# DLRM on one core: filling the gram's slots from the PSUM bank of the transposes in place of the features in SBUF

## The chip, the cores and the metric

The kernel runs on 1 core of a Trainium2 chip. The metric is the time of one execution on the device in microseconds. A run with the profiler gives, beside its time, the span of the profiled instructions.

## What is computed

A recommendation model (DLRM) for 2048 samples: 26 rows are looked up in embedding tables for each sample, a small network gives a 27th vector, the products of all pairs of the 27 vectors are taken, and all of it goes through four dense layers.

```python
B, NF, D, V, NDENSE = (2048, 26, 64, 12500, 13)
h = jax.nn.relu(dense @ dw1 + db1)
dense_emb = jax.nn.relu(h @ dw2 + db2)
sparse_emb = emb_tables[f_ids, sparse_idx]
emb = jnp.concatenate([dense_emb[:, None, :], sparse_emb], axis=1)
inter = jnp.einsum('bfd,bgd->bfg', emb, emb)
pairs = inter[:, iu0, iu1]
z = jnp.concatenate([emb.reshape(emb.shape[0], -1), pairs], axis=1)
z = jax.nn.relu(z @ ow1 + ob1)
z = jax.nn.relu(z @ ow2 + ob2)
z = jax.nn.relu(z @ ow3 + ob3)
return z @ ow4 + ob4
```

## The kernel before

The 2048 samples are 16 tiles of 128. All five engines run one program each, written out by hand; semaphores order them, and within an engine the order of the code is the order of the work.

**GpSimd** issues the gathers (line 212): 26 indirect DMAs a tile, one for each table, each bringing 128 rows of 64 floats into `emb`, a ring of four tiles. Two neighbouring tables lie side by side, so a tile is 13 blocks of 128x128. The blocks are in four groups (`GROUPS`: 4, 4, 4 and 1 blocks), each with its semaphore. Before the gathers of tile t GpSimd waits for the transposes of group 0 of tile t-1.

**TensorE** waits for a group's rows, transposes its blocks (line 540) into `tr_ps`, which has two PSUM banks: groups 0 and 2 use bank 0, groups 1 and 3 bank 1. The features, now 128 features x 128 samples a block, are the weights of layer 1 (line 588, `features1`), which accumulates in `l1_ps`. `gram` (line 567) multiplies samples' slots with themselves for the products. `turn_pairs` transposes the picked pairs of the tile before through bank 0 of `tr_ps`, `pairs1` adds them to layer 1, `turn_hidden1` transposes the layer's result. `upper(b, s)` are the steps of layers 2 to 4 for a batch of tiles and use bank 1 of `tr_ps`. The last tile, 15, has its own order (lines 709 to 736) and its own forms: `last_features1` (line 656), `last_gram` (line 635).

**Evacuation.** ScalarE copies groups 0 and 2 out of `tr_ps` into `feat` (`evac_features`, line 375), VectorE groups 1 and 3 (line 247). For the gram the features are needed a second time, in another layout: `slots[h*64 + d, j, c, f]`, where the 128 samples are split in (c, h, j) and the 27 slots f are next to each other, padded to 32. Slots 0 to 12 are the lower halves (features 0 to 63) of the 13 blocks, slots 13 to 25 the upper halves, slot 26 the dense vector. ScalarE fills the first from `feat` (`even_slots`, line 382), VectorE the second (`odd_slots`, line 254), each in two parts of a tile (`SLOT_PARTS`: blocks 0 to 7 and 8 to 12; three parts in the last tile). A part is two copies, one for each h; each reads single floats that are 128 apart in `feat` and writes runs of as many floats as the part has blocks. Line 434 fills the dense slot.

**Around it.** After the gram ScalarE (line 394) and VectorE (line 278) copy it out of PSUM, VectorE transposes it in 32x32 blocks (line 286; the last tile's straight from PSUM, line 298), ScalarE picks the pairs (`pick_pairs`, lines 400 and 406). `hidden1_turn` (line 266) is VectorE's copy of layer 1's turned result. `result(b)` (line 428) is ScalarE's last step of a batch; `hidden2`, `hidden3` are the ones before.

The semaphores `feat_act` and `feat_dve` count the evacuations, `slots_act` and `slots_dve` the slot parts. TensorE waits for `feat_act` or `feat_dve` before it writes a bank of `tr_ps` again (line 531 in `transposes`, and in `turn_pairs` and `upper`), and for the slots before `gram`.

Of the kernel before, what the change touches and what calls it, by code (L numbers as in the profile page):

```python
# [13 lines left out]
P = 128  # L14
# [1 line left out]
GROUPS = [(0, 4), (4, 8), (8, 12), (12, 13)]  # L16
BATCHES = [(0, 4), (4, 8), (8, 12), (12, 14), (14, 15), (15, 16)]
LAST = BATCHES[-1][0]
SLOT_PARTS = [(0, 8), (8, 13)]
LAST_PARTS = [(0, 8), (8, 12), (12, 13)]  # L20


def bass_dlrm_kernel(
# [18 lines left out]
    D = dw1.shape[1]  # L42
# [21 lines left out]
    with ExitStack() as ctx:  # L64
# [153 lines left out]
        def _(dve):  # L218
# [24 lines left out]
            def evac_features(t, n):  # L243
                a, b = GROUPS[n]
                src = tr_ps[:, n % 2, 0:(b - a) * P].rearrange("p (k c) -> p k c", c=P)
                dve.wait_ge(transposed, t * NG + n + 1)
                nc.vector.tensor_copy(feat[t % 2][:, a:b, :], src).then_inc(feat_dve, 1)  # L247

            def odd_slots(t, a, b):
                dve.wait_ge(feat_act, 2 * t + (1 if b <= 8 else 2))  # L250
                dve.wait_ge(feat_dve, 2 * t + (1 if b <= 12 else 2))
                for h in range(2):
                    src = feat[t % 2][D:P, a:b].rearrange("p k (c h j) -> p h j c k", h=2, j=HALF)[:, h]
                    last = nc.vector.tensor_copy(slots[t % 2][h * D:(h + 1) * D, :, :, NP + a:NP + b], src)  # L254
                last.then_inc(slots_dve, 1)

            def pairs_copy(t):
# [60 lines left out]
            for t in range(LAST):  # L318
                if t >= 1:
                    gram_copies(t - 1, 0)  # L320
                    if end_stage(t - 1) and end_stage(t - 1)[1] == 1:
                        hidden2(end_stage(t - 1)[0])
                    gram_copies(t - 1, 1)
                    turn_gram(t - 1)
                    pairs_copy(t - 1)
                evac_features(t, 1)
                if t >= 1:
                    hidden1_turn(t - 1)
                odd_slots(t, *SLOT_PARTS[0])
                if mid_stage(t) and mid_stage(t)[1] == 1:  # L330
                    hidden2(mid_stage(t)[0])
                evac_features(t, 3)
                odd_slots(t, *SLOT_PARTS[1])
            gram_copies(14, 0)
            gram_copies(14, 1)
            turn_gram(14)
            hidden2(3)
            pairs_copy(14)
            evac_features(15, 1)
            hidden1_turn(14)  # L340
            odd_slots(15, *LAST_PARTS[0])
            odd_slots(15, *LAST_PARTS[1])
            evac_features(15, 3)
            odd_slots(15, *LAST_PARTS[2])
            turn_last_gram()
            pick_high_pairs()
            pairs_copy(15)
# [4 lines left out]
        def _(act):  # L352
# [21 lines left out]
                act.wait_ge(transposed, t * NG + n + 1)  # L374
                nc.scalar.copy(feat[t % 2][:, a:b, :], src).then_inc(feat_act, 1)  # L375

            def even_slots(t, a, b):
                act.wait_ge(feat_act, 2 * t + (1 if b <= 8 else 2))
                act.wait_ge(feat_dve, 2 * t + (1 if b <= 12 else 2))
                for h in range(2):  # L380
                    src = feat[t % 2][0:D, a:b].rearrange("p k (c h j) -> p h j c k", h=2, j=HALF)[:, h]
                    last = nc.scalar.copy(slots[t % 2][h * D:(h + 1) * D, :, :, a:b], src)  # L382
                last.then_inc(slots_act, 1)

            def gram_copies(t, half):
# [89 lines left out]
            for t in range(LAST):  # L475
                if t >= 1:
                    gram_copies(t - 1, 0)
                    if end_stage(t - 1):
                        upper_act(*end_stage(t - 1))
                    gram_copies(t - 1, 1)  # L480
                evac_features(t, 0)
                if t >= 1:
                    pick_pairs(t - 1)
                    hidden1(t - 1)
                dense_slots(t)
                even_slots(t, *SLOT_PARTS[0])
                if mid_stage(t):
                    upper_act(*mid_stage(t))
                evac_features(t, 2)
                even_slots(t, *SLOT_PARTS[1])  # L490
            gram_copies(14, 0)
            hidden2(3)
            gram_copies(14, 1)
            evac_features(15, 0)
            pick_pairs(14)
            hidden1(14)
            dense_slots(15)
            even_slots(15, *LAST_PARTS[0])
            hidden3(3)
            evac_features(15, 2)  # L500
            result(3)
            even_slots(15, *LAST_PARTS[1])
            even_slots(15, *LAST_PARTS[2])
            pick_low_pairs()
            hidden2(4)
            last_hidden1(0)
# [8 lines left out]
        def _(pe):  # L515
# [12 lines left out]
            def transposes(t, n):  # L528
                a, b = GROUPS[n]
                if 2 * t + n // 2 > 0:  # L530
                    pe.wait_ge((feat_act, feat_dve)[n % 2], 2 * t + n // 2)
                if n == 1 and t >= 1 and end_stage(t - 1):
                    pe.wait_ge(upper_out, out_count(end_stage(t - 1)))
                if n == 2 and t >= 1:
                    pe.wait_ge(pairs_in, t)
                if n == 3 and mid_stage(t):
                    pe.wait_ge(upper_out, out_count(mid_stage(t)))
                pe.wait_ge(gathered[t % RING][n], (t // RING + 1) * 32 * (b - a))
                for k in range(a, b):
                    last = nc.tensor.transpose(tr_ps[:, n % 2, (k - a) * P:(k - a + 1) * P], emb[:, t % RING, k, :],  # L540
                                               ident_sb[:])
                last.then_inc(transposed, 1)

            def turn_pairs(t, evacuated):
                pe.wait_ge(feat_act, evacuated)
                if t == LAST:
                    pe.wait_ge(last_picked, 2)
                else:
                    pe.wait_ge(pairs_picked, t + 1)
                for c in range(PC):  # L550
                    mm = nc.tensor.transpose(tr_ps[0:PR, 0, c * P:(c + 1) * P],  # L551
                                             pairs_b[t % 2][:, c * PR:(c + 1) * PR], ident_sb[:])
                mm.then_inc(pairs_turned, 1)

            def gram(t, half):
                if half == 0:
                    pe.wait_ge(dense_slot, t + 1)
                    pe.wait_ge(slots_act, len(SLOT_PARTS) * (t + 1))
                    pe.wait_ge(slots_dve, len(SLOT_PARTS) * (t + 1))
                if 2 * t + half > 0:  # L560
                    pe.wait_ge(gram_act, 2 * t + half)
                    pe.wait_ge(gram_dve, 2 * t + half)
                for j in range(half * HALF // 2, (half + 1) * HALF // 2):
                    for h in range(2):
                        x = slots[t % 2][h * D:(h + 1) * D, j]
                        bank, r = 2 * h + j // SETS % 2, j % SETS
                        mm = nc.tensor.matmul(gram_ps[:, bank, r * GCOLS:(r + 1) * GCOLS],  # L567
                                              x.rearrange("p c f -> p (c f)"), x[:, :, 0:SLOTS],
                                              start=True, stop=True)
                mm.then_inc(gram_done, 1)  # L570
# [33 lines left out]

            def upper(b, s, evacuated):
                n = upper_cols(b)
                pe.wait_ge(feat_dve, evacuated)
                if b + s > 0:
                    pe.wait_ge(upper_out, 4 * b + s)
                if s == 0:  # L610
                    pe.wait_ge(h1t_ready, BATCHES[b][1])
                    if b == 0:
                        pe.wait_ge(w234_in, 48)
                if s in (0, 1):
                    for k in range(M1):
                        mm = nc.tensor.matmul(tr_ps[:, 1, 0:n], w2_sb[:, k, s * P:(s + 1) * P], h1t[b % 2][:, k, 0:n],  # L616
                                              start=(k == 0), stop=(k == M1 - 1))
                    mm.then_inc(l2_done, 1)
                elif s == 2:
                    for k in range(M2):  # L620
                        mm = nc.tensor.matmul(tr_ps[:, 1, 0:n], w3_sb[:, k, :], h2[:, k, 0:n],
                                              start=(k == 0), stop=(k == M2 - 1))
                    mm.then_inc(l3_done, 1)
                else:
                    nc.tensor.matmul(tr_ps[0:1, 1, 0:n], w4_sb[:], h3[:, 0:n], start=True, stop=True).then_inc(l4_done, 1)

            def last_gram():
                pe.wait_ge(dense_slot, LAST + 1)
                pe.wait_ge(slots_act, len(SLOT_PARTS) * LAST + len(LAST_PARTS))
                pe.wait_ge(slots_dve, len(SLOT_PARTS) * LAST + len(LAST_PARTS))  # L630
                for j in range(HALF):
                    for c in range(SETS):
                        for h in range(2):
# [169 lines left out]
```

## Time and profile before

| | us |
|---|---|
| median of 3 runs | 552.72 |
| lowest, highest | 552.71, 553.63 |
| the profiled execution | 554.64 |
| its span | 552.7 |
| TensorE busy (matmul) | 444.2 |
| GpSimd busy | 398.2 |
| ScalarE busy | 159.4 |
| VectorE busy | 141.9 |

Busy time is what an engine's instructions cover; the issuing of a gather on GpSimd counts as busy. The granted TensorE clock of the execution was 0.928 of full speed. A row of the timeline starts with its start and its length in us. An engine that waits names in brackets who released it; "issue" means that nothing in the profile held it. An fp32 matmul of the program stands as two in the trace.

### The profile page before, as it was taken

Reading aid. Unit: us, or ns where it says so; the run is one execution under the profiler, and the core shown is the slowest. Engines: PE = TensorE matmul, PEld = TensorE weight load, DVE = VectorE, ACT = ScalarE, POOL = GpSimd, SP = SyncE. Lnnn points to the kernel's source line nnn. Section 1 sums busy time; section 2 is a strip of 40 time slices with the busy share of each in tenths; the row PEclk is TensorE's granted clock in tenths of the full one; section 3 lists DMA queues with packets and bytes.
Section 4 is the critical chain, followed back from the end, with each engine's and each line's share of the span. In section 5 each row is a group of like instructions: output and inputs, shape, how many; then the busy total and the mean of one; then the engine's idle time right before and its main releaser. Section 6 shows DMA issues by size and latency. Waiting matters only on the chain.

```text
span 552.7 us, 5884 instructions
## 1 busy us (share of the span) xinstructions
PE 444.2 (80%) x2326; PEld 236.6 (43%) x2326; DVE 141.9 (26%) x225; ACT 159.4 (29%) x265; POOL 398.2 (72%) x420
## 2 busy tenths in 40 slices
PE   3757989585887979799685988979597899959978
PEld 1124553252534435354342534525253444525767
DVE  1003324031331223214032231413222123311412
ACT  1303334122232232324133232323333223332322
POOL 5777777777777777777777777777777777777720
PEclk9999999798898979979798998979989799997998
DMA  8633323233332323333232332324333232333310
GB/s 274 133 49 25 29 26 25 27 28 26 27 26 26 27 26 28 26 27 26 26 28 26 27 26 28 27 26 27 26 28 26 26 27 26 27 25 27 26 13 1
DMA packets 17166, 19.38 MB, mean 35 GB/s; under 512 B 7359, under 2 KB 8386, under 8 KB 17127
## 3 DMA queue, kind: packets, MB, share of 16 engines
q0 software_dynamic: 13312, 13.66, 30.5%
q1 hardware_dynamic: 3408, 5.02, 2.7%
q10 hardware_dynamic: 420, 0.34, 0.3%
q8 instruction: 18, 0.29, 0.2%
q14 instruction: 8, 0.07, 0.0%
HBM read 18.99 MB, written 0.01 MB: 34 GB/s over the span
## 4 chain that ended last, share of the span: by engine, by line
POOL 57%; issue 19%; PE 15%; DMA 6%; SPq 1%; ACT 1%; DVE 1%; POOLq 0%; DVEq 0%
POOL emb L212 57%; DMA w1p_sb<-ow_pairs_dram 5%; PE l_ps L588 5%; PE gram_ps L567 2%; PE tr_ps L616 2%; PE l_ps L656 1%; DMA emb<-table_dram,rows 1%; PE gram_ps L656 1%; PE tr_ps L540 1%; PE l_ps L594 1%; PE gram_ps L635 0%; SPq L189 0%; PE l_ps L581 0%; PE gram_ps L663 0%; PE l_ps L663 0%
## 5 line engine op out<-in xcount | busy, mean ns | idle before, releaser
L212 POOL DMA_INDIRECT emb<-table_dram,rows x416 | 398.0, 957 | 130.1 <-issue 125.6
L588 PE MATMUL l_ps<-w_sb,feat 128*128 128x512 f32 x390 | 204.3, 674 | 3.7 <-DVE feat L247 1.5
L588 PEld LDWEIGHTS l_ps<-w_sb,feat 128*128 128x128 f32 x390 | 81.8, 220 | 107.6 <-issue 89.8
L540 PE MATMUL tr_ps<-ident_sb,emb 128*128 128x128 f32 x208 | 39.3, 306 | 62.5 <-DMA emb<-table_dram,rows 61.4
L278 DVE COPY gram_c<-gram_ps 32x432 f32<-32x432 f32 x60 | 36.6, 610 | 138.8 <-PE gram_ps L567 138.4
L382 ACT COPY slots<-feat 64x512 f32<-64x512 f32 (+3 forms) x66 | 58.6, 888 | 45.6 <-DVE feat L247 43.6
L567 PEld LDWEIGHTS gram_ps<-slots 64*128 64x128 f32 x960 | 56.1, 188 | 26.8 <-issue 15.5
L567 PE MATMUL gram_ps<-slots 64*128 64x108 f32 x960 | 61.2, 277 | 6.7 <-DVE gram_c L278 6.7
L394 ACT COPY gram_c<-gram_ps 32x432 f32<-32x432 f32 x60 | 30.6, 509 | 122.4 <-PE gram_ps L567 122.0
L247 DVE COPY feat<-tr_ps 128x512 f32<-128x512 f32 (+1 forms) x32 | 15.7, 492 | 191.4 <-PE tr_ps L540 191.4
L540 PEld LDWEIGHTS tr_ps<-ident_sb,emb 128*128 128x128 f32 x208 | 26.1, 152 | 90.2 <-issue 88.7
L594 PE MATMUL l_ps<-w1p_sb,pairs 118*128 118x512 f32 x90 | 42.6, 610 | 9.8 <-DVE pairs L259 9.8
L375 ACT COPY feat<-tr_ps 128x512 f32<-128x512 f32 x32 | 18.8, 586 | 77.9 <-PE tr_ps L540 77.6
L254 DVE COPY slots<-feat 64x512 f32<-64x512 f32 (+3 forms) x66 | 34.6, 524 | 6.8 <-ACT feat L375 4.2
L411 ACT ACTIVATE h<-l_ps 128x512 f32<-128x512 f32 x15 | 9.0, 598 | 74.5 <-PE l_ps L594 74.5
L616 PE MATMUL tr_ps<-h1t,w_sb 128*128 128x512 f32 (+2 forms) x80 | 28.6, 502 | 0.2 <-ACT h L416 0.2
L286 DVE STREAM_TRANSPOSE gram_b<-gram_c 128x864 f32<-128x864 f32 x15 | 28.1, 1872 | 1.4
L594 PEld LDWEIGHTS l_ps<-w1p_sb,pairs 118*128 118x128 f32 x90 | 15.9, 189 | 27.7 <-issue 14.4
L581 PE MATMUL l_ps<-w1d_sb,dense_e 64*128 64x512 f32 x30 | 17.8, 674 | 8.2 <-DMA w1p_sb<-ow_pairs_dram 8.2
L259 DVE COPY pairs<-tr_ps 118x384 f32<-118x384 f32 x16 | 8.9, 558 | 41.3 <-PE tr_ps L551 41.3
L616 PEld LDWEIGHTS tr_ps<-h1t,w_sb 128*128 128x128 f32 x80 | 14.0, 197 | 10.6 <-issue 9.5
L518 PE MATMUL gram_ps<-dense_sb,dw_sb 13*64 13x512 f32 x8 | 7.1, 1063 | 9.0 <-DMA dw_sb<-dw_dram 9.0
(67 smaller groups left out, 174.9 us busy)
## 6 DMA issues: line engine op xcount, KB each, us to landing
emb<-table_dram,rows POOLq DMA_INDIRECT x416, 3.3
w_sb<-ow_dram SPq DMA_DIRECT2D x3, 1024.0 KB, 9.7
w1p_sb<-ow_pairs_dram SPq DMA_DIRECT2D x1, 708.0 KB
w_sb<-ow_dram SPq DMA_DIRECT2D x1, 512.0 KB, 21.8
w_sb<-ow_dram SPq DMA_DIRECT2D x1, 256.0 KB, 13.0
idx_raw<-idx_dram ACTq DMA_DIRECT2D x1, 208.0 KB, 2.6
w1d_sb<-ow_dram SPq DMA_DIRECT2D x1, 128.0 KB
w_sb<-ow_dram SPq DMA_DIRECT2D x1, 128.0 KB, 6.4
```

What stands on the lines that cost most here:

```text
L212: pool.indirect_dma_start(out=emb[:, t % RING, c // 2, c % 2 * D:(c % 2 + 1) * D], out_offset=None, in_=table, in_offset=bass.IndirectOffs ...
L254: last = nc.vector.tensor_copy(slots[t % 2][h * D:(h + 1) * D, :, :, NP + a:NP + b], src)
L278: last = nc.vector.tensor_copy(dst, src)
L286: nc.vector.transpose(gram_b[t % 2][:, 0:SLOTS, :], gram_c[:].rearrange("p i g -> p g i")).then_inc(gram_turned, 1)
L375: nc.scalar.copy(feat[t % 2][:, a:b, :], src).then_inc(feat_act, 1)
L382: last = nc.scalar.copy(slots[t % 2][h * D:(h + 1) * D, :, :, a:b], src)
L394: last = nc.scalar.copy(dst, src)
L540: last = nc.tensor.transpose(tr_ps[:, n % 2, (k - a) * P:(k - a + 1) * P], emb[:, t % RING, k, :], ident_sb[:])
L567: mm = nc.tensor.matmul(gram_ps[:, bank, r * GCOLS:(r + 1) * GCOLS], x.rearrange("p c f -> p (c f)"), x[:, :, 0:SLOTS], start=True, stop=True)
L588: nc.tensor.matmul(l1_ps[t % 2][:], feat[t % 2][:, n - 1, :], w1_sb[:, n - 1, :], start=False, stop=False)
L594: mm = nc.tensor.matmul(l1_ps[t % 2][:], pairs[t % 2][:, c, :], w1p_sb[:, c, :], start=False, stop=c == PC - 1)
L616: mm = nc.tensor.matmul(tr_ps[:, 1, 0:n], w2_sb[:, k, s * P:(s + 1) * P], h1t[b % 2][:, k, 0:n], start=(k == 0), stop=(k == M1 - 1))
```

## The change

`even_slots` and `odd_slots` are gone, and with them their two parts a tile. In their place stands `group_slots(t, n)`, once on ScalarE and once on VectorE, called right behind `evac_features(t, n)` for the same group. It makes four copies out of the bank of `tr_ps` that was just evacuated: for each half of the partitions (even and odd slots) and each h one. So ScalarE fills all slots of groups 0 and 2, VectorE all of groups 1 and 3. What is read lies again 128 floats apart, now in PSUM; what is written are runs of 4 floats (of 1 in group 3).

TensorE therefore waits for `slots_act` and `slots_dve` where it waited for `feat_act` and `feat_dve` before it writes a bank of `tr_ps`. Layer 1 (`features1`, `last_features1`) still waits for `feat_act` and `feat_dve`. The gram waits for two groups of each engine. TensorE's and GpSimd's instructions and their order stay.

```diff
--- before.py
+++ after.py
@@ -16,8 +16,6 @@
 GROUPS = [(0, 4), (4, 8), (8, 12), (12, 13)]
 BATCHES = [(0, 4), (4, 8), (8, 12), (12, 14), (14, 15), (15, 16)]
 LAST = BATCHES[-1][0]
-SLOT_PARTS = [(0, 8), (8, 13)]
-LAST_PARTS = [(0, 8), (8, 12), (12, 13)]
 
 
 def bass_dlrm_kernel(
@@ -246,12 +244,13 @@
                 dve.wait_ge(transposed, t * NG + n + 1)
                 nc.vector.tensor_copy(feat[t % 2][:, a:b, :], src).then_inc(feat_dve, 1)
 
-            def odd_slots(t, a, b):
-                dve.wait_ge(feat_act, 2 * t + (1 if b <= 8 else 2))
-                dve.wait_ge(feat_dve, 2 * t + (1 if b <= 12 else 2))
-                for h in range(2):
-                    src = feat[t % 2][D:P, a:b].rearrange("p k (c h j) -> p h j c k", h=2, j=HALF)[:, h]
-                    last = nc.vector.tensor_copy(slots[t % 2][h * D:(h + 1) * D, :, :, NP + a:NP + b], src)
+            def group_slots(t, n):
+                a, b = GROUPS[n]
+                for half, base in ((0, a), (1, NP + a)):
+                    src = tr_ps[half * D:(half + 1) * D, n % 2, 0:(b - a) * P].rearrange(
+                        "p (k c h j) -> p h j c k", k=b - a, h=2, j=HALF)
+                    for h in range(2):
+                        last = nc.vector.tensor_copy(slots[t % 2][h * D:(h + 1) * D, :, :, base:base + b - a], src[:, h])
                 last.then_inc(slots_dve, 1)
 
             def pairs_copy(t):
@@ -324,24 +323,23 @@
                     turn_gram(t - 1)
                     pairs_copy(t - 1)
                 evac_features(t, 1)
+                group_slots(t, 1)
                 if t >= 1:
                     hidden1_turn(t - 1)
-                odd_slots(t, *SLOT_PARTS[0])
                 if mid_stage(t) and mid_stage(t)[1] == 1:
                     hidden2(mid_stage(t)[0])
                 evac_features(t, 3)
-                odd_slots(t, *SLOT_PARTS[1])
+                group_slots(t, 3)
             gram_copies(14, 0)
             gram_copies(14, 1)
             turn_gram(14)
             hidden2(3)
             pairs_copy(14)
             evac_features(15, 1)
+            group_slots(15, 1)
             hidden1_turn(14)
-            odd_slots(15, *LAST_PARTS[0])
-            odd_slots(15, *LAST_PARTS[1])
             evac_features(15, 3)
-            odd_slots(15, *LAST_PARTS[2])
+            group_slots(15, 3)
             turn_last_gram()
             pick_high_pairs()
             pairs_copy(15)
@@ -374,12 +372,13 @@
                 act.wait_ge(transposed, t * NG + n + 1)
                 nc.scalar.copy(feat[t % 2][:, a:b, :], src).then_inc(feat_act, 1)
 
-            def even_slots(t, a, b):
-                act.wait_ge(feat_act, 2 * t + (1 if b <= 8 else 2))
-                act.wait_ge(feat_dve, 2 * t + (1 if b <= 12 else 2))
-                for h in range(2):
-                    src = feat[t % 2][0:D, a:b].rearrange("p k (c h j) -> p h j c k", h=2, j=HALF)[:, h]
-                    last = nc.scalar.copy(slots[t % 2][h * D:(h + 1) * D, :, :, a:b], src)
+            def group_slots(t, n):
+                a, b = GROUPS[n]
+                for half, base in ((0, a), (1, NP + a)):
+                    src = tr_ps[half * D:(half + 1) * D, n % 2, 0:(b - a) * P].rearrange(
+                        "p (k c h j) -> p h j c k", k=b - a, h=2, j=HALF)
+                    for h in range(2):
+                        last = nc.scalar.copy(slots[t % 2][h * D:(h + 1) * D, :, :, base:base + b - a], src[:, h])
                 last.then_inc(slots_act, 1)
 
             def gram_copies(t, half):
@@ -479,28 +478,27 @@
                         upper_act(*end_stage(t - 1))
                     gram_copies(t - 1, 1)
                 evac_features(t, 0)
+                group_slots(t, 0)
                 if t >= 1:
                     pick_pairs(t - 1)
                     hidden1(t - 1)
                 dense_slots(t)
-                even_slots(t, *SLOT_PARTS[0])
                 if mid_stage(t):
                     upper_act(*mid_stage(t))
                 evac_features(t, 2)
-                even_slots(t, *SLOT_PARTS[1])
+                group_slots(t, 2)
             gram_copies(14, 0)
             hidden2(3)
             gram_copies(14, 1)
             evac_features(15, 0)
+            group_slots(15, 0)
             pick_pairs(14)
             hidden1(14)
             dense_slots(15)
-            even_slots(15, *LAST_PARTS[0])
             hidden3(3)
             evac_features(15, 2)
+            group_slots(15, 2)
             result(3)
-            even_slots(15, *LAST_PARTS[1])
-            even_slots(15, *LAST_PARTS[2])
             pick_low_pairs()
             hidden2(4)
             last_hidden1(0)
@@ -528,7 +526,7 @@
             def transposes(t, n):
                 a, b = GROUPS[n]
                 if 2 * t + n // 2 > 0:
-                    pe.wait_ge((feat_act, feat_dve)[n % 2], 2 * t + n // 2)
+                    pe.wait_ge((slots_act, slots_dve)[n % 2], 2 * t + n // 2)
                 if n == 1 and t >= 1 and end_stage(t - 1):
                     pe.wait_ge(upper_out, out_count(end_stage(t - 1)))
                 if n == 2 and t >= 1:
@@ -542,7 +540,7 @@
                 last.then_inc(transposed, 1)
 
             def turn_pairs(t, evacuated):
-                pe.wait_ge(feat_act, evacuated)
+                pe.wait_ge(slots_act, evacuated)
                 if t == LAST:
                     pe.wait_ge(last_picked, 2)
                 else:
@@ -555,8 +553,8 @@
             def gram(t, half):
                 if half == 0:
                     pe.wait_ge(dense_slot, t + 1)
-                    pe.wait_ge(slots_act, len(SLOT_PARTS) * (t + 1))
-                    pe.wait_ge(slots_dve, len(SLOT_PARTS) * (t + 1))
+                    pe.wait_ge(slots_act, 2 * t + 2)
+                    pe.wait_ge(slots_dve, 2 * t + 2)
                 if 2 * t + half > 0:
                     pe.wait_ge(gram_act, 2 * t + half)
                     pe.wait_ge(gram_dve, 2 * t + half)
@@ -604,7 +602,7 @@
 
             def upper(b, s, evacuated):
                 n = upper_cols(b)
-                pe.wait_ge(feat_dve, evacuated)
+                pe.wait_ge(slots_dve, evacuated)
                 if b + s > 0:
                     pe.wait_ge(upper_out, 4 * b + s)
                 if s == 0:
@@ -626,8 +624,8 @@
 
             def last_gram():
                 pe.wait_ge(dense_slot, LAST + 1)
-                pe.wait_ge(slots_act, len(SLOT_PARTS) * LAST + len(LAST_PARTS))
-                pe.wait_ge(slots_dve, len(SLOT_PARTS) * LAST + len(LAST_PARTS))
+                pe.wait_ge(slots_act, 2 * LAST + 2)
+                pe.wait_ge(slots_dve, 2 * LAST + 2)
                 for j in range(HALF):
                     for c in range(SETS):
                         for h in range(2):
```

On VectorE, in tile 1 of the program, before (`COPY slots<-feat` is `odd_slots`, `h1t` is `hidden1_turn`):

```order
L247 COPY feat<-tr_ps 128x512
L266 COPY h1t<-l_ps 128x4x128
L254 COPY slots<-feat 64x64x8 x2
L247 COPY feat<-tr_ps 128x128
L254 COPY slots<-feat 64x64x5 x2
```

and now:

```order
L245 COPY feat<-tr_ps 128x512
L253 COPY slots<-tr_ps 64x64x4 x4
L265 COPY h1t<-l_ps 128x4x128
L245 COPY feat<-tr_ps 128x128
L253 COPY slots<-tr_ps 64x64 x4
```

The copies read `tr_ps`, there are eight and not four, and `hidden1_turn` stands behind the first four.

On ScalarE, in the last tile, before (`COPY gram_b` and `pairs_b` are `pick_pairs(14)`, `ACTIVATE y` is `result(3)`, the `ACTIVATE h` of 128x256 is `hidden3(3)`):

```order
L375 COPY feat<-tr_ps 128x512
L400 COPY gram_b<-gram_b 128x13x13
L406 COPY pairs_b<-gram_b 128x351
L411 ACTIVATE h_0<-l_ps 128x512
L434 COPY slots<-dense_e 64x64 x2
L382 COPY slots<-feat 64x64x8 x2
L422 ACTIVATE h<-tr_ps,bias_sb 128x256
L375 COPY feat<-tr_ps 128x512
L428 ACTIVATE y<-tr_ps,bias_sb 1x256
L382 COPY slots<-feat 64x64x4 x2
L382 COPY slots<-feat 64x64 x2
```

and now:

```order
L373 COPY feat<-tr_ps 128x512
L381 COPY slots<-tr_ps 64x64x4 x4
L399 COPY gram_b<-gram_b 128x13x13
L405 COPY pairs_b<-gram_b 128x351
L410 ACTIVATE h_0<-l_ps 128x512
L433 COPY slots<-dense_e 64x64 x2
L421 ACTIVATE h<-tr_ps,bias_sb 128x256
L373 COPY feat<-tr_ps 128x512
L381 COPY slots<-tr_ps 64x64x4 x4
L427 ACTIVATE y<-tr_ps,bias_sb 1x256
```

`pick_pairs(14)` and `result(3)` each stand behind four copies that were not ahead of them. TensorE's next step after `result(3)` are the transposes of group 3 of tile 15.

## Rows read from the trace of the kernel before

**Rows 1.** Page, part 1: busy time of each engine (share of the span) and instructions

```profile
PE 444.2 (80%) x2326; PEld 236.6 (43%) x2326; DVE 141.9 (26%) x225; ACT 159.4 (29%) x265; POOL 398.2 (72%) x420
```

**Rows 2.** Line L212, the gathers: duration ns min/median/max; and issue to landing

```profile
L212 POOL DMA_INDIRECT emb<-table_dram,rows x416: 941/947/1377, 4.1 to 527.6; - x139
...
DMA to landing us min/median/max: 2.4/3.3/6.4
```

**Rows 3.** Waits: who waited for whom, us in total, times, longest

```profile
PE tr_ps L540 <- DMA emb<-table_dram,rows: 61.4, 27, 5.1
...
POOL emb L212 <- PE tr_ps L540: 0.9, 3, 0.3
```

**Rows 4.** Timeline, POOL: start us, us, what, [idle before <-releaser]; four gathers

```profile
4.07 1.08 POOL L212 DMA_INDIRECT emb<-table_dram,rows  x1 [3.62 <-DVE rows L234]
...
494.69 0.95 POOL L212 DMA_INDIRECT emb<-table_dram,rows  x1 [0.30 <-issue]
...
507.36 0.94 POOL L212 DMA_INDIRECT emb<-table_dram,rows  x1 [0.30 <-issue]
...
522.36 0.95 POOL L212 DMA_INDIRECT emb<-table_dram,rows  x1 [0.30 <-issue]
```

**Rows 5.** Timeline: the first and the last long gather after a copy into slots began

```profile
42.61 0.59 DVE L254 COPY slots<-feat 64x512 f32<-64x512 f32 x1
...
42.98 1.04 POOL L212 DMA_INDIRECT emb<-table_dram,rows  x1 [0.30 <-issue]
...
524.63 1.23 DVE L254 COPY slots<-feat 64x512 f32<-64x512 f32 x2
...
524.86 1.20 POOL L212 DMA_INDIRECT emb<-table_dram,rows  x1 [0.30 <-issue]
```

**Rows 6.** Timeline: a gather beside the transpose of `gram_c` on VectorE

```profile
317.23 1.87 DVE L286 STREAM_TRANSPOSE gram_b<-gram_c 128x864 f32<-128x864 f32 x1
...
317.74 0.95 POOL L212 DMA_INDIRECT emb<-table_dram,rows  x1 [0.31 <-issue]
```

**Rows 7.** Groups by line and form: count, busy us, mean ns; line 254 from the page

```profile
L382 ACT COPY slots<-feat 64x256 f32<-64x256 f32 x2 | 1.2, 622 | 0.0
...
L458 ACT ACTIVATE h1t<-l_ps 128x256 f32<-128x256 f32 x1 | 0.4, 384 | 2.6 <-PE l_ps L663 2.6
...
L254 DVE COPY slots<-feat 64x512 f32<-64x512 f32 (+3 forms) x66 | 34.6, 524 | 6.8 <-ACT feat L375 4.2
...
L278 DVE COPY gram_c<-gram_ps 32x432 f32<-32x432 f32 x60 | 36.6, 610 | 138.8 <-PE gram_ps L567 138.4
...
L247 DVE COPY feat<-tr_ps 128x128 f32<-128x128 f32 x16 | 4.7, 292 | 103.3 <-PE tr_ps L540 103.3
...
L298 DVE STREAM_TRANSPOSE gram_b<-gram_ps 128x864 f32<-128x864 f32 x1 | 1.1, 1084 | 6.2 <-PE gram_ps L635 6.2
```

**Rows 8.** Timeline, last tile: ACT, DVE and PE rows on which the tail rests

```profile
498.10 0.45 PE L540 MATMUL tr_ps<-ident_sb,emb 128*128 128x128 f32 x1 [1.80 <-DMA emb<-table_dram,rows]
...
513.89 0.59 ACT L375 COPY feat<-tr_ps 128x512 f32<-128x512 f32 x1 [1.32 <-PE tr_ps L540]
...
515.14 0.81 ACT L406 COPY pairs_b<-gram_b 128x351 f32<-128x351 f32 x1
...
518.44 0.35 PEld L551 LDWEIGHTS tr_ps<-ident_sb,pairs_b 128*118 128x118 f32 x3
...
529.24 0.59 ACT L375 COPY feat<-tr_ps 128x512 f32<-128x512 f32 x1 [0.27 <-PE tr_ps L540]
...
529.76 0.47 ACT L428 ACTIVATE y<-tr_ps,bias_sb 1x256 f32<-1x256 f32 x1
...
531.66 0.14 PEld L540 LDWEIGHTS tr_ps<-ident_sb,emb 128*128 128x128 f32 x1
...
532.08 0.29 DVE L247 COPY feat<-tr_ps 128x128 f32<-128x128 f32 x1 [1.44 <-PE tr_ps L540]
...
533.75 1.95 PE L635 MATMUL gram_ps<-slots 64*32 64x27 f32 x208
```

## The prediction

> **What bounds the kernel now.** First the busy shares of the page: TensorE is busy for 80% of the span, GpSimd for 72%, ScalarE and VectorE for less than 30% [rows 1]. That would point at TensorE. Then the waits: TensorE's transposes of line 540 waited 27 times, 61.4 us in all, for gathered rows to land, and the gathers never waited for a transpose longer than 0.3 us, which is their normal gap [rows 3]. So the gathers pace the kernel. They leave GpSimd one after the other: 416 of them, 947 ns as the median and 1377 ns at most [rows 2], and between 507.36 and 522.36 twelve steps take 15.00 us, 1.25 us each [rows 4]. Sixteen tiles of 26 gathers are 520 us of the 552.7. TensorE, ScalarE and VectorE work inside that stream and have time left in every tile.
>
> The chain of waits tells where this stops being so. Its last gather starts at 494.69 [rows 4], the last one of tile 14. It lands about 3.3 us later [rows 2], TensorE transposes the rows at 498.10 [rows 8], and from there to the end at 552.7 TensorE's own order is what counts: the rest of tile 14, then tile 15 while its rows are already there when they are wanted. So the span is made of two parts: the stream of gathers up to 494.69, and a tail of 54.6 us from 498.10.
>
> **What the change does to the stream.** The gathers are not all equally long. From 4.07 to 494.69 [rows 4] lie 389 steps. The 388 steps of the whole stream that are shorter than 1.27 us have a mean of 1.2504 us; 389 of those make 486.4 us, and 490.6 were taken. The excess is 4.2 us. Of it 0.14 is the very first gather (1.08 us, rows 4), beside which VectorE works on the indices; this stays. The other 4.1 us sit in 24 gathers of 0.98 to 1.38 us (two more lie in tile 15). The timeline shows what they have in common: in each of these 26 a VectorE copy into `slots`, line 254, is running. The first begins at 42.98 beside a copy of 42.61, the last at 524.86 and takes 1.20 us beside copies of 524.63 [rows 5]. No other VectorE work does that. The 15 transposes of `gram_c` run for 1.87 us each, 33 gathers overlap with them and none is long, as at 317.74 [rows 6]; the 60 copies of line 278 out of PSUM [rows 7] overlap with 55 gathers, none is long. The same holds for the copies out of PSUM of lines 247, 266 and 259, save where a copy of line 254 runs in the same gather.
>
> Line 254 is the one plain copy on VectorE that reads SBUF and writes SBUF inside the stream. The change takes out all 66 of these copies and reads the same values from PSUM. What is read is then of the kind of lines 278 and 247, which leave the gathers alone. I take it that all 4.1 us go: tile 14's last gather then starts at 490.6. The unknown is whether reading SBUF is what does it, or writing the stepped `slots`; the new copies still write those. Both ends are in the rivals.
>
> **What it does to ScalarE and VectorE.** Before, ScalarE fills the even half of the slots and VectorE the odd half, each from `feat`. Now whoever evacuates a group makes four copies of it. On ScalarE a tile has eight copies of 64x256 in place of four larger ones. Their price is not in the trace: a stepped read of SBUF takes 622 ns for 64x256, a packed read of PSUM takes 384 ns for 128x256 [rows 7]. They lie between those two, so four of them are 1.5 to 2.5 us. Which is nearer? On VectorE the transposes of 864 elements take 1.87 us where they read SBUF with a step of 27 elements [rows 6] and 1084 ns where they read PSUM with a step of 32 [rows 7], which is the pace of packed PSUM reads: from 292 ns at 128 to 610 ns at 432 elements [rows 7] it is 1.05 ns each. A step costs nothing there in PSUM. I take 384 ns, so 1.5 us for four.
>
> The Trainium skill speaks against this: the page "SBUF — State Buffer", section on the door 1 port swizzle, says that SBUF keeps full bandwidth only while accesses fall in the same 16-byte line and that PSUM's lines are 8 bytes. By it, a step of 512 bytes in PSUM would be slow as well. The VectorE row above disagrees, and no row here has ScalarE reading PSUM with a step; so that price is a rival.
>
> On VectorE four copies of group 1 cost at the PSUM pace 292 + 128 x 1.05 = 426 ns each, 1.7 us; the four 64x64 copies of group 3 cost at most 292 each and about 226 by the same pace, 0.9 us.
>
> In tiles 0 to 14 all this is covered. TensorE waits in every tile for the rows of groups 2 and 3, 61.4 us over 27 waits [rows 3], so a microsecond that a copy holds `tr_ps` longer comes out of that wait. No gather waits for it either: the gate of a tile's gathers is the first transpose group of the tile before, and no wait on it is longer than a gap [rows 3]. The cover ends at 498.10.
>
> **The tail, place by place.** (a) `pick_pairs(14)` now stands behind the four copies of group 0: the evacuation of 513.89 ends at 514.48, the copies at 516.0, the picks (before they ended at 515.95) at 517.2. TensorE loads them at 518.44 [rows 8]. Covered, even at 622 ns, when they end at 518.2. (b) `hidden1_turn(14)` on VectorE comes 1.7 us later; the next to need it is the batch of tile 14 after `last_gram`, over 10 us on. Nothing. (c) `result(3)` now stands behind the four copies of group 2. The evacuation ends at 529.83; before, the result ran at 529.76 for 0.47 us [rows 8]. Now it ends at 529.83 + 1.5 + 0.47 = 531.8. TensorE must have it before the transpose of group 3, whose weights are loaded at 531.66 [rows 8]. That is 0.2 us of a new wait. (d) `last_gram` needs all slots. From the load at 531.66 VectorE starts its evacuation 0.42 us later (532.08), takes 0.29, then the four copies 0.9: all done 1.65 us after the load; TensorE started at 533.75, 2.09 us after it [rows 8]. Covered, and just so at 292 ns each (1.9 us). (e) the rest is unchanged.
>
> **Sum.** Span 552.7 - 4.1 + 0.2 = 548.8 us. The profiled execution took 554.64 us in all, the median of the runs shown is 552.72 and its neighbour 552.71; I apply the difference of -3.9 us to the median: **548.8 us**.
>
> **Rivals.**
> ScalarE reads stepped PSUM at the SBUF price: (c) becomes 529.83 + 2.5 + 0.47 = 532.8, a wait of 1.2 us in place of 0.2. The median is 549.8. This is the outcome by the page's lines. For it speaks only that ScalarE's price is not shown.
> Half of the stretching stays, because writing the stepped `slots` holds the gathers up as well: 552.7 - 2.05 + 0.2, **550.9**. Against it: long gathers appear with line 254 and nothing else, but line 254 is also the only line of VectorE that writes `slots` in the stream, so the two causes are not apart in this trace.
> All of it stays (the read has no part in it) and the copies are as long in sum as before: 552.9.
> The other side: the write alone is the cause, and the copies are longer. VectorE's slot copies per tile go from 2.2 us (34.6 us in 16 tiles [rows 7]) to 2.6, and at 292 ns for the small ones to 2.9 us. Then the 4.1 us grow by a third to 5.4, and with (c) at 1.2 it is 552.7 + 1.3 + 1.2 = **555.2**. It decides for slower from the point at which the stretch and the tail together add 1.1 us. I know no cheaper way to a loss: the tail alone would need ScalarE copies of 1.4 us each to eat the gain.
>
> **How the numbers follow.** Forecast 548.8: 0.55. ScalarE at the SBUF price, 549.8: 0.22. Half stays, 550.9: 0.10. All stays, 552.9: 0.05. Slower, 555.2: 0.08. The low end is below the forecast by what I can't price (the gather of 524.86 is no longer long, and (c) may be hidden whole): 547.8. The high end takes in the half: 551.2. Some 0.2% (1.1 us) is about what a measurement of this kernel can tell from no change, so faster means below 551.6: 0.87; within: 0.05; slower: 0.08.
>
> **What would show it.** In the profile after: line 210 (the gathers) with a maximum near 1.08 us and a busy sum of 394 in place of 398 us; the last gather of tile 14 near 490.6. The 64x256 group of ScalarE's new line 381 near 384 ns, or near 622 for the first rival; the group of VectorE's line 253 near 430. In the tail the load of group 3's transpose 0.2 us later in relation to the transpose of 498.10, with `y` as what it waited for. If gathers are still long beside line 253, the write is the cause and the forecast is wrong; if the gathers are even but the span hasn't moved by 4 us, the tail has taken it and the place is (c) or (d).

## The result, and the profile after

The changed kernel took 549.87 us as the median of 4 runs (548.94 to 550.04), the kernel before beside it 553.17 us (552.71 to 553.96): ratio 0.9933, 95% interval 0.9914 to 0.9952. On another chip, with 5 runs, it was 548.4 against 552.96 us, ratio 0.991 (0.9894 to 0.9927). It is faster by 3.3 to 4.6 us; the forecast was 3.9.

The changed kernel, as in [rows 1, 2, 7]: busy time of each engine from the page; the durations of the gathers, ns min/median/max; the slot copies by form, count | busy us, mean ns | idle before.

```profile
PE 441.0 (81%) x2326; PEld 235.5 (43%) x2326; DVE 148.8 (27%) x287; ACT 148.8 (27%) x327; POOL 393.1 (72%) x420
```

```profile
L210 POOL DMA_INDIRECT emb<-table_dram,rows x416: 940/945/1079, 4.1 to 522.5; - x139
```

```profile
L381 ACT COPY slots<-tr_ps 64x256 f32<-64x256 f32 x128 | 51.0, 399 | 1.1
...
L253 DVE COPY slots<-tr_ps 64x256 f32<-64x256 f32 x64 | 27.2, 425 | 0.7
L253 DVE COPY slots<-tr_ps 64x64 f32<-64x64 f32 x64 | 16.7, 261 | 0.6
```

The longest gather is 1079 ns, where it was 1377 [rows 2], and GpSimd's busy time has gone from 398.2 to 393.1 us. That longest one is the first of the kernel; not one of the other 415 is above 0.96 us. VectorE is busy for 7 us more than before and ScalarE for 11 us less, and neither matters.

The end of the stream and the start of the tail, from the timeline, as in [rows 4, 8]:

```profile
490.02 0.94 POOL L210 DMA_INDIRECT emb<-table_dram,rows  x1 [0.30 <-issue]
...
493.41 0.45 PE L538 MATMUL tr_ps<-ident_sb,emb 128*128 128x128 f32 x1 [1.58 <-DMA emb<-table_dram,rows]
```

Tile 14's last gather starts at 490.02 and not at 494.69, 4.7 us sooner. 4.1 of it are the long gathers: beyond equal steps the stream took 4.21 us up to that gather before and 0.14 us now. The other 0.6 us are the equal steps themselves, 1.2487 us where they were 1.2504; over the traces shown below they lie between 1.2481 and 1.2508 whatever the kernel, so this part is not the change's.

### The profile page after: what moved, and what is told of

The parts are those of the page before. It is cut to its first block, busy times and chain, and to the rows that moved or that the text cites. A ratio compares the mean times of both kernels' runs of the same rounds, so it can differ in the third digit from the quotient of the medians.

```text
span 547.5 us, 5942 instructions
## 1 busy us (share of the span) xinstructions
PE 441.0 (81%) x2326; PEld 235.5 (43%) x2326; DVE 148.8 (27%) x287; ACT 148.8 (27%) x327; POOL 393.1 (72%) x420
## 4 chain that ended last, share of the span: by engine, by line
POOL 66%; issue 22%; PE 9%; DMA 2%; POOLq 0%; ACT 0%; DVE 0%
POOL emb L210 66%; PE l_ps L586 2%; PE tr_ps L614 2%; DMA emb<-table_dram,rows 2%; PE gram_ps L565 1%; PE tr_ps L538 1%; PE l_ps L654 1%; PE gram_ps L654 0%; PE gram_ps L633 0%; DMA first_sb<-first_dram 0%; PE gram_ps L661 0%; PE l_ps L661 0%; POOLq L62 0%; PE l_ps L671 0%; PE gram_ps L671 0%
## 5 line engine op out<-in xcount | busy, mean ns | idle before, releaser
L210 POOL DMA_INDIRECT emb<-table_dram,rows x416 | 392.9, 944 | 130.1 <-issue 125.8
L586 PE MATMUL l_ps<-w_sb,feat 128*128 128x512 f32 x390 | 201.2, 666 | 3.8 <-DVE feat L245 1.5
L586 PEld LDWEIGHTS l_ps<-w_sb,feat 128*128 128x128 f32 x390 | 80.7, 217 | 105.6 <-issue 87.6
L381 ACT COPY slots<-tr_ps 64x256 f32<-64x256 f32 x128 | 51.0, 399 | 1.1
L253 DVE COPY slots<-tr_ps 64x256 f32<-64x256 f32 (+1 forms) x128 | 43.9, 343 | 1.3
```

The source lines that it names most:

```text
L210: pool.indirect_dma_start(out=emb[:, t % RING, c // 2, c % 2 * D:(c % 2 + 1) * D], out_offset=None, in_=table, in_offset=bass.IndirectOffs ...
L586: nc.tensor.matmul(l1_ps[t % 2][:], feat[t % 2][:, n - 1, :], w1_sb[:, n - 1, :], start=False, stop=False)
```

## The experiments

**VectorE's copies read SBUF again.** The changed kernel with this edit on VectorE:

```diff
 def group_slots(t, n):
     a, b = GROUPS[n]
+    dve.wait_ge(feat_dve, 2 * t + n // 2 + 1)
     for half, base in ((0, a), (1, NP + a)):
-        src = tr_ps[half * D:(half + 1) * D, n % 2, 0:(b - a) * P].rearrange(
+        src = feat[t % 2][half * D:(half + 1) * D, a:b].rearrange(
```

> The changed kernel, but VectorE's eight slot copies a tile read `feat` in SBUF again and not `tr_ps`; ScalarE's stay on PSUM. Theory read (VectorE holds gathers up when a plain copy has both ends in SBUF): the long gathers come back, with 4 x 380 + 4 x 230 ns = 2.4 us of such copies a tile against 2.2 before; 4 to 5 us in excess up to tile 14's last gather, the time near 553.5 to 554. Rival (what held the gathers up was the split by halves or the size of the copies): gathers stay at 0.94 us, time 549.9.

> As e1_dve_from_sbuf: the changed kernel with VectorE's slot copies read from `feat`. Where the gathers pace the kernel: theory read says that the even gathers are the whole gain, so that without them the time is that of the kernel before less what the tail gained, ratio 0.998 to 1.003. Rival (the gain comes from elsewhere, from the earlier clock of tile 14 or the copies' order): ratio 0.993 to 0.996 with long gathers.

The first was run on a chip on which this kernel and the one before both take about 760 us (more on that below), so its time (ratio 0.9964, 0.9936 to 0.9992) says nothing of the gathers, but its trace does: 15 gathers beside line 254 above 0.96 us, up to 1128 ns. On a chip like that of the rows: ratio 0.9969 (0.9955 to 0.9983), 551.75 us, and 17 long gathers besides the first, 1.5 us of excess up to tile 14's last gather. One of them in its timeline:

```profile
41.74 1.57 DVE L254 COPY slots<-feat 64x256 f32<-64x256 f32 x4
...
42.98 1.15 POOL L210 DMA_INDIRECT emb<-table_dram,rows  x1 [0.30 <-issue]
```

The gathers are long again, and only beside these copies. The size was expected wrong: an excess of 4 to 5 us was on record and 1.5 came back, and the ratio of 0.9969 is in neither of the recorded ranges (0.998 to 1.003 for the theory, 0.993 to 0.996 for the rival). So this run shows that these copies bring long gathers back, about a third of them by excess, and not that they are the whole gain. What counts is not the copies' sum but where they fall in a gather, and these are shorter and stand elsewhere in the tile: before, the fourth gather of 11 of the 16 tiles lost 0.16 to 0.21 us beside the second slot part; now that place holds only 64x64 copies and no gather there is long.

**ScalarE's copies read SBUF again**, the same edit on ScalarE (`act.wait_ge(feat_act, ...)`, `feat`):

> The changed kernel, but ScalarE's eight slot copies a tile read `feat` in SBUF; VectorE's stay on PSUM. Theory read: no long gather but the first, since ScalarE does not hold them up. ScalarE's copies take 622 ns and not 399, so `result(3)` ends 0.9 us later and the transpose of group 3 in the last tile waits about 0.9 us more: time 550.8. Rival (the gain was partly ScalarE's: its SBUF reads held gathers up too): long gathers come back, 552 to 554.

> As e2_act_from_sbuf: the changed kernel with ScalarE's slot copies read from `feat` at 632 ns. Where the gathers pace the kernel: even gathers, and `result(3)` in the last tile 0.9 us later: ratio 0.995, 0.9 us above the changed kernel. Rival: no difference to the changed kernel, since the wait in the last tile is covered.

In both traces the gathers stay even (the longest is the first, 1079 and 1080 ns). So ScalarE doesn't hold them up, whatever it reads. The first run was made on the chip with 760 us: ratio 1.0044 (1.0022 to 1.0065), slower than the kernel before. The second, on the other chip: ratio 0.994 (0.9923 to 0.9957), 550.16 us. Its copies and the last tile:

```profile
L382 ACT COPY slots<-feat 64x256 f32<-64x256 f32 x128 | 80.8, 631 | 2.1
```

```profile
525.28 2.56 ACT L382 COPY slots<-feat 64x256 f32<-64x256 f32 x4
...
527.86 0.47 ACT L428 ACTIVATE y<-tr_ps,bias_sb 1x256 f32<-1x256 f32 x1
528.38 0.33 PE L539 MATMUL tr_ps<-ident_sb,emb 128*128 128x128 f32 x1 [1.03 <-ACT y L428]
```

Here the wait that the prediction put at (c) is seen by name: TensorE stood 1.03 us for `y`, `result(3)`. A copy that takes 631 ns and not 399 makes TensorE stand for 1 us at this one place. In the other fifteen tiles it holds up no gather: tile 14's last one starts at 490.33, in the two traces of the changed kernel at 490.02 and 490.41. What the wait is worth in the kernel's time is less sure: the medians on that chip differ by 1.8 us where 0.9 was expected, and their intervals just meet.

**The stepped write doubled, without a read of SBUF.** In tiles 0 to 14 VectorE repeats its four copies into a spare tensor:

```diff
+ if t < LAST:
+     if t + n > 1:
+         dve.wait_ge(slots_dve, 2 * t + n // 2)
+     ...
+             last = nc.vector.tensor_copy(
+                 spare[h * D:(h + 1) * D, :, :, base:base + b - a], src[:, h])
  last.then_inc(slots_dve, 1)
```

> The changed kernel with VectorE's slot copies made twice in tiles 0 to 14, the second time into a spare tensor of the same layout, still from `tr_ps`: the stepped writing of SBUF doubled, no SBUF read added. Theory read: all gathers even, time 549.9 within 0.5. Rival (stepped writes hold gathers up, only too little to be seen): some gathers above 0.96 us and an excess of over 0.5 us.

Run on the chip with 760 us. 248 copies out of PSUM into the stepped layout, and no gather but the first is above 0.96 us; this answers the question that the trace of before left open. The write has no part in it. The changed kernel's own trace says the same: in 21 of its gathers a slot copy of VectorE out of PSUM runs at a place at which line 254 held every gather before (see the last section), and none of the 21 is long. The time was not to be read there (ratio 1.0019, 0.9993 to 1.0044, to the kernel before).

**Copies that nothing needs, packed, from SBUF to SBUF.** Behind each slot group of tiles 0 to 14, on VectorE:

```diff
  last.then_inc(slots_dve, 1)
+ if t < LAST:
+     ...
+     for i in range(2):
+         last = nc.vector.tensor_copy(spare[:, i], w1_sb[:, 2 * i:2 * i + 2, :].rearrange("p k n -> p (k n)"))
```

> The changed kernel with two VectorE copies of 128x1024 packed floats from SBUF to a spare SBUF tensor behind each of its slot groups in tiles 0 to 14 (60 copies, nothing else waits for them but VectorE's next work). Theory both ends in SBUF: gathers that begin beside them are long although nothing is stepped; 60 copies of some 0.6 us are about the 35 us of copies of before, so an excess of about 4 us or more, time 553 to 556. Rival (only stepped reads do it): gathers even, time 549.9 to 550.5.

> As e5_packed_sbuf, the changed kernel with 60 more VectorE copies of 128x1024 packed floats from SBUF to SBUF that nothing needs. Where the gathers pace the kernel, theory: long gathers beside them as in e5 (34 of them, 5.1 us in sum), the excess up to tile 14's last gather is some 4 to 5 us and the whole kernel is later by just that: ratio 0.998 to 1.003 to the kernel before, 4 to 5 us above the changed one. Rival (the excess of gathers isn't time, the kernel has other slack): ratio 0.993.

On the chip with 760 us: 34 long gathers besides the first. On the other: ratio 1.0041 (1.0026 to 1.0057), 555.22 us against 553.19, with 46 long gathers besides the first and 5.9 us of excess. So no step of the reading is needed for it either. The ratio is above the recorded 0.998 to 1.003, and 5.9 us are more than the expected 4 to 5. On the chip with 760 us the ratio was 1.0025 (0.9997 to 1.0052). In the timeline of the second:

```profile
196.67 1.30 DVE L262 COPY spare<-w_sb 128x1024 f32<-128x1024 f32 x2
196.95 1.23 POOL L212 DMA_INDIRECT emb<-table_dram,rows  x1 [0.30 <-issue]
198.00 0.69 DVE L274 COPY h1t<-l_ps 128x512 f32<-128x512 f32 x1
198.48 0.94 POOL L212 DMA_INDIRECT emb<-table_dram,rows  x1 [0.30 <-issue]
```

The copy of `h1t` out of PSUM that follows leaves its gather alone.

**The gain without reading PSUM.** The kernel before, with VectorE's slot copies given to ScalarE, all from `feat`:

```diff
 def even_slots(t, a, b):
     ...
     last.then_inc(slots_act, 1)
+    for h in range(2):
+        src = feat[t % 2][D:P, a:b].rearrange("p k (c h j) -> p h j c k", h=2, j=HALF)[:, h]
+        last = nc.scalar.copy(slots[t % 2][h * D:(h + 1) * D, :, :, NP + a:NP + b], src)
+    last.then_inc(slots_dve, 1)
```

> The kernel before with one edit: ScalarE makes VectorE's slot copies too, all still read from `feat` in SBUF; no copy reads `tr_ps` for the slots. Theory (only VectorE's plain copies with both ends in SBUF cost gathers time, and that is the whole gain of the change): every gather but the first even, 4.1 us less of stream; the last tile's slots are done 0.2 us after TensorE wants them, as 4 x 622 and 4 x 304 ns stand on ScalarE behind 530.2. Ratio 0.991 to 0.994, like the change. Rival (reading PSUM in itself, or the group-wise order, gave a part): ratio 0.996 or more.

Ratio 0.994 (0.9916 to 0.9964), 550.12 us; one long gather, the first. Nothing of the change is in this kernel but that VectorE makes no slot copy from SBUF, and it has nearly all of the gain: 3.1 us, where the change had 3.3 and 4.6. ScalarE's sum of slot copies is twice what it was, and what that costs stands once in the last tile:

```profile
528.83 1.94 PE L626 MATMUL gram_ps<-slots 64*32 64x27 f32 x208 [0.31 <-ACT slots L373]
```

0.31 us, where 0.2 were expected.

**`result(3)` first.** The changed kernel with one line moved:

```diff
 evac_features(15, 2)
-group_slots(15, 2)
 result(3)
+group_slots(15, 2)
```

> The changed kernel with `result(3)` ahead of `group_slots(15, 2)` on ScalarE, one line moved. The wait of the last tile's group 3 transpose goes, 0.2 us; the slots of group 2 are done 0.5 us later, about 1 us ahead of `last_gram`. Expected: 0.2 us less than the changed kernel, which the runs can't tell from nothing; in the trace the transpose of group 3 comes 0.12 us sooner after the features ahead of it.

> The changed kernel once more, beside the two experiments that go with it, on one chip. Where the gathers pace the kernel, as in the traces of before and after: ratio 0.993 to the kernel before. Where TensorE's instructions come too slowly, as in the four runs so far (holes of 1 to 2 us between single matmuls of the gram, 760 us): the even gathers give nothing, since GpSimd waits there for TensorE once a tile; ratio 0.998 to 1.002.

The transpose of group 3 starts 1.89 us after the features ahead of it (526.64 and 524.75), as before the change, and 2.01 us in the changed kernel (526.98 and 524.97): the 0.12 us are there. The time was 549.56 us, ratio 0.9926 (0.9908 to 0.9945), beside 548.4 and 0.991 for the changed kernel on the same chip; the intervals overlap, and a gain of that size can't be told. No version of the study is faster than the changed kernel.

**Excess and time.** The runs on the chips where the gathers pace the kernel, by the excess of the gathers up to tile 14's last one:

| kernel | gathers above 0.96 us | excess, us | ratio to before |
|---|---|---|---|
| changed | 1 | 0.13 | 0.991 |
| changed, `result(3)` first | 1 | 0.13 | 0.9926 |
| changed, ScalarE from SBUF | 1 | 0.16 | 0.994 |
| before, slot copies all on ScalarE | 1 | 0.13 | 0.994 |
| changed, VectorE from SBUF | 18 | 1.5 | 0.9969 |
| before | 27 | 4.2 | 1 |
| changed, 60 packed copies more | 47 | 5.9 | 1.0041 |

The kernels with more excess have the higher ratios; the first four differ in the ratio and not in the excess. From the changed kernel to the last row the excess grows by 5.8 us and the ratio by 0.0131, which is 7.2 us; the two intervals allow 5.5 to 9.0. On one chip, from the kernel with all slot copies on ScalarE to the last row, it is 5.8 us of excess and 5.1 us of time (3.4 to 7.8). So a microsecond of excess is about a microsecond of the kernel. The row with 18 long gathers fits least well: 1.4 us of excess more than the changed kernel, but 3.3 us of time, of which the intervals allow 1.5 to 4.9. What else that kernel loses, if anything, was not found.

## Why the prediction was right

- **The gathers pace the kernel, and long gathers are its loss.** Right, and shown from both sides: taken away by the change and by another edit, brought back by two, though by one of them only in part.
- **All 4.1 us go.** Right: 4.07 us of excess less (4.21 to 0.14). The open question, read or write, was settled for the first by the doubled write; the rivals in which the write keeps half, or all, or makes it worse (550.9, 552.9, 555.2) fall together.
- **ScalarE reads stepped PSUM at the packed price.** 384 ns was taken, 399 measured [rows 7 for the 384], against 631 from SBUF. The row that decided it was VectorE's transpose out of PSUM. That it carried over to another engine was a guess with no row of ScalarE behind it, and some luck. What the prediction drew from the Trainium skill ("SBUF — State Buffer", the section on door 1, whose words on PSUM speak of matmuls) would have given a slow read; the measurement decides against that for these two engines. The first comparison (3.3 us less) lies between the forecast (3.9 less) and this rival (2.9 less), so the time doesn't part the two; the 399 ns do. The run with 631 ns shows what that rival would have been: 1.03 us of wait at (c), ratio 0.994 on the chip where the change has 0.991.
- **VectorE's prices.** 426 ns taken for 64x256, 425 measured; 226 taken for 64x64, 261 measured. So (d) had 0.14 us less room than thought and still held: the slots were done at 528.65, `last_gram` began at 529.03.
- **(a), (b).** Covered, as said. `pick_pairs(14)` ended 1.2 us before TensorE's transposes wanted it.
- **(c).** 0.2 us forecast. In the trace `y` ends at 526.93 and the transpose starts at 526.98; it comes 0.12 us later after the features ahead of it than before, and the features behind it 0.18 us (2.18 us after 524.97, where it was 2.00):

```profile
524.33 0.59 ACT L373 COPY feat<-tr_ps 128x512 f32<-128x512 f32 x1 [1.55 <-PE tr_ps L538]
524.81 1.63 ACT L381 COPY slots<-tr_ps 64x256 f32<-64x256 f32 x4
524.97 0.71 PE L654 MATMUL l_ps<-feat,w_sb 128*128 128x128 f32 x4 [0.15 <-ACT feat L373]
...
526.46 0.47 ACT L427 ACTIVATE y<-tr_ps,bias_sb 1x256 f32<-1x256 f32 x1
526.98 0.33 PE L538 MATMUL tr_ps<-ident_sb,emb 128*128 128x128 f32 x1
```

- **"Its rows are already there when they are wanted."** This half of the picture of the tail was too simple. Up to `last_gram` the tail has two bounds that lie close: TensorE's own work from tile 14's last rows on, and the gathers of tile 15's group 2, the last but two of the kernel. Before, TensorE came to the transposes of group 2 at 528.57 straight from its own work. In the profiled run after it was the gathers:

```profile
523.66 0.63 PE L538 MATMUL tr_ps<-ident_sb,emb 128*128 128x128 f32 x4 [1.40 <-DMA emb<-table_dram,rows]
```

The reason is TensorE's clock. The ten matmuls of features behind tile 14's last rows took 7.29 us before and 5.79 us now; the granted clock of those stretches was 0.61 and 0.77 of full speed, that is, part of them ran at 1.2 GHz and part at 2.4, after TensorE had waited some 3.6 us for rows in both. The 1.5 us won there were handed over almost whole to the wait of 1.40 us. In the second profile of the changed kernel the same matmuls took 7.26 us, and TensorE did not wait at that place. So when the clock rises moves the tail's inner times by 1.5 us and the end hardly at all (from tile 14's last gather to the end it is 57.4 us with the early rise and 57.8 with the late one), while a microsecond off the gathers moves both bounds and is kept. It doesn't change the sum, and it is why the profiled pair of before and after must not be read as 552.7 less 547.5: of these 5.2 us, 4.7 are the stream's; the rest is the changes of the clock, the wait, (c), and a hole of TensorE inside `last_gram`, 2.64 us before and 2.02 after, which lies between 1.99 and 2.68 us in all the traces of chips like this.

## What to carry to other kernels

Where gathers issued by GpSimd pace a kernel, look at the spread of their durations before their mean, and at what VectorE runs inside the long ones: here plain VectorE copies from SBUF to SBUF cost 4 us of 553 though VectorE was idle for three quarters of the time. Reading the same values from PSUM, or giving the copies to ScalarE, took that away; a stepped read out of PSUM cost next to nothing extra on either engine (399 ns against 384 on ScalarE, 425 against 426 on VectorE). Then look for the one place at the end of the kernel where a step now stands behind the longer copies, since nothing covers it there.

## What the hardware showed

**How long a gather is held.** A gather takes 0.94 us when nothing holds it, and VectorE's copy from SBUF to SBUF holds it only at certain places. From the trace of before:

```profile
46.82 0.95 POOL L212 DMA_INDIRECT emb<-table_dram,rows  x1 [0.30 <-issue]
...
47.35 1.01 DVE L254 COPY slots<-feat 64x320 f32<-64x320 f32 x2 [0.22 <-ACT feat L375]
48.08 1.12 POOL L212 DMA_INDIRECT emb<-table_dram,rows  x1 [0.30 <-issue]
```

The two copies begin 0.53 us into the first gather and outlast it, and it is not long. They end at 48.37, 0.29 us into the second, and that one ends at 49.20, 0.83 us after them. Three rules fit all the long gathers beside such copies, 26 in the trace of before, 17 in that with VectorE from SBUF and 46 in that with the packed copies:

- A copy that is already running when the gather begins and ends 0.14 us or more into it: the gather ends 0.80 to 0.84 us after that copy. This is so for 21, 15 and 30 of them. The longest gather, 1.38 us from 488.01, is of this kind: its copy ends 0.55 us into it. So is the one at 196.95 above.
- A copy that begins 0.2 to 0.50 us into the gather and ends 0.84 us or more into it: the gather ends 0.12 us after that copy. This is so for the other 5, 2 and 16. (At 0.51 to 0.52 us is the edge: of three copies that began there, one did this and is counted here, two did not.)
- A copy that begins within 0.03 us of the gather's start, or 0.53 us or more into it, does not make it long.

So the gather is held at two points, for as long as the copy that is then running, and not slowed down on the whole: in the trace of before 58 gathers overlapped with copies of line 254, and 26 of them were long. The hold goes the other way too: of the packed copies, which take 0.69 us as a rule, the eight that began 0.53 to 0.66 us into a gather took 0.80 to 0.93 us. The Trainium skill, "SBUF — State Buffer", section "Who interferes with whom", says that VectorE's copies in a mode with two ports lock GpSimd out for a whole instruction. The trace agrees for a copy that is running at one of the two points; no row names the mode in which a copy ran.

The pace of a copy is a weak sign of the kind that holds. 128x1024 packed from SBUF to SBUF takes 713 ns, 0.70 ns an element; VectorE's copies out of PSUM take 1.05 ns for each further element. But the stepped copies of line 254, 608 ns for 64x512 and 380 for 64x256, take 0.89 for each further element and held gathers all the same. The transposes of line 286 also read and write SBUF, 1.87 us each, and held none of the 33 gathers beside them.

**A chip on which TensorE stands between single matmuls.** Four of the runs above were made on a chip on which the kernel before takes 761.74 us (31 runs, 756.46 to 770.12) and the variants 759 to 764. Their profiles show where the time goes, though not why. In the gram of a tile single matmuls stand apart, here with VectorE from SBUF:

```profile
428.07 0.25 PE L566 MATMUL gram_ps<-slots 64*128 64x108 f32 x1 [1.37 <-issue]
430.17 0.26 PE L566 MATMUL gram_ps<-slots 64*128 64x108 f32 x1 [1.85 <-issue]
```

and in the same trace the gathers wait for TensorE, 182 us in 14 waits, where they waited 0.9 us [rows 3]:

```profile
POOL emb L210 <- PE tr_ps L539: 182.4, 14, 22.0
```

TensorE waits there for nothing that the profile shows. It looks like the hole inside `last_gram`, a dense stretch of short matmuls, on the other chips. One recorded expectation above puts it down to instructions that come too slowly; that was not tested, and the cause is open. The changed kernel itself was not run on that chip; where the gathers wait for TensorE, even gathers should give nothing, which no run shows.
